# A GRU stack with a feed-forward stage: the feed-forward features by tokens for a whole batch, its weights made in pieces during the stack, the first fusions among the last tails

## What is computed

```python
def _mingru(x, Wz, bz, Wh, bh):
    z = sigmoid(einsum('bsi,hi->bsh', x, Wz) + bz)
    h_tilde = tanh(einsum('bsi,hi->bsh', x, Wh) + bh)
    return _linear_scan(clip(1.0 - z, 1e-8, 1.0 - 1e-8), z * h_tilde)
# 4 layers: h = layernorm(_mingru(h) + (h if i > 0 else 0), gamma, beta); Wz = Wh = ctx[i], bz = bh = cond[i]
x = x + fusion(concat(forward stack, flip(backward stack)))        # 1024 -> 512, of layernorm(x)
gamma = mean(abs(W)) + 1e-6
absmean(W) = sign(W / gamma) * minimum(round(abs(W / gamma)), 1)   # -1, 0 or 1
h = gelu(einsum('btd,hd->bth', layernorm(x), absmean(W_fc)))       # 512 -> 2048
x = x + einsum('bth,dh->btd', layernorm(h, ln_w, ln_b), absmean(W_proj))
```

## Time and profile before

| | |
|---|---|
| median of 3 runs | 1803.64 us (1803.44 to 1804.62) |
| the profiled execution | 1806.48 us |
| its span, first to last instruction | 1804.1 us |
| mean granted TensorE clock | 0.966 |
| TensorE, VectorE, ScalarE, GpSimd busy | 92%, 73%, 53%, 44% of the span |
| the GRU stack's products | 28 to 1009 us |
| first product of `fc` | 1097 us |

### The profile page before, as it was taken

One profiled execution on the slowest core, in us unless ns is written; L12 is line 12 of the kernel. 1 busy time (PEld: TensorE's weight loads), 2 busy tenths in 40 slices (PEclk: granted clock), 3 DMA queues, 4 the chain that ended last, 5 costly groups with the idle time before them and its releaser, 6 DMA issues.

```text
span 1804.1 us, 24288 instructions
## 1 busy us (share of the span) xinstructions
PE 1660.4 (92%) x8448; PEld 1365.1 (76%) x8448; DVE 1324.2 (73%) x2405; ACT 959.5 (53%) x1588; POOL 798.8 (44%) x842
## 2 busy tenths in 40 slices
PE   4779999999799999999999449999999999999999
PEld 3768787877678778777777336888888888888887
DVE  3678889898689989899899468666555555555565
ACT  4367888988578788887977302222222222222222
POOL 2247776767567678675777334111111111111110
PEclk9789999999899999999999768999999999999999
DMA  4000121200010100101001252111111111111100
GB/s 175 1 1 13 36 96 40 100 30 13 21 50 24 48 1 1 71 24 54 1 13 59 85 172 64 47 48 47 47 49 51 49 49 51 50 53 49 48 30 18
DMA packets 62727, 84.67 MB, mean 47 GB/s; under 512 B 3984, under 2 KB 36752, under 8 KB 60432
## 3 DMA queue, kind: packets, MB, share of 16 engines
q1 hardware_dynamic: 58144, 75.01, 12.5%
q10 hardware_dynamic: 4464, 8.13, 1.5%
HBM read 57.95 MB, written 25.17 MB: 46 GB/s over the span
## 4 chain that ended last, share of the span: by engine, by line
PE 56%; DVE 19%; ACT 13%; POOL 6%; issue 5%; DMA 1%; SPq 0%; POOLq 0%; ACTq 0%; DVEq 0%
PE ps L460 13%; PE ps L431 13%; PE ps L333 11%; PE ps L405 10%; DVE bnp L691 4%; ACT ntok L536 4%; PE ps L447 3%; DVE AL L706 3%; ACT H L558 3%; POOL rsp L968 2%; PE ps L367 2%; POOL hb L951 2%; DVE zb L673 2%; ACT AH L563 2%; DVE ps L660 2%
## 5 line engine op out<-in xcount | busy, mean ns | idle before, releaser
L333 PE MATMUL ps<-AH,WH 128*128 128x512 f32 x896 | 373.3, 417 | 29.6 <-DVE AL L706 15.5
L951 POOL TENSOR_TENSOR hb<-zb,hb 128x512 f32<-128x512 f32 x224 | 291.5, 1302 | 145.6 <-ACT hb L525 145.5
L333 PE MATMUL ps<-AL,WH 128*128 128x512 f32 x896 | 354.9, 396 | 0.0
L333 PE MATMUL ps<-AH,WL 128*128 128x512 f32 x896 | 354.4, 396 | 0.0
L673 DVE TENSOR_TENSOR_SCAN zb<-ps,hb 128x512 f32<-128x512 f32 x192 | 234.2, 1220 | 49.0 <-POOL hb L951 43.6
L960 POOL TENSOR_TENSOR H<-H,zb 128x512 f32<-128x512 f32 x192 | 247.9, 1291 | 18.5 <-DVE zb L673 11.7
L629 ACT ACTIVATE uth<-ps 128x512 fp32r<-128x512 f32 x128 | 72.9, 596 | 327.4 <-PE ps L447 327.4
L884 DVE TENSOR_TENSOR utl<-ps,uth 128x512 fp32r<-128x512 f32 x128 | 85.4, 689 | 190.4 <-ACT uth L629 190.3
L333 PEld LDWEIGHTS ps<-AH,WH 128*128 128x128 f32 x896 | 171.6, 192 | 68.4 <-DVE AL L706 17.0
L536 ACT ACTIVATE ntok<-ps,nbp,rsp 128x512 f32<-128x512 f32 x256 | 185.8, 781 | 66.2 <-POOL nbp L971 65.7
L367 PE MATMUL ps<-ident,ntok 128*128 128x128 f32 x1152 | 170.2, 285 | 45.1 <-ACT ntok L536 24.1
(11 more groups left out here) (119 smaller groups left out, 3268.9 us busy)
## 6 DMA issues: line engine op xcount, KB each, us to landing
hs_scratch<-H SPq DMA_DIRECT2D x16, 1024.0 KB, 4.9
hc<-hs_scratch SPq DMA_DIRECT2D x32, 512.0 KB, 4.3
xr<-in_x SPq DMA_DIRECT2D x32, 256.0 KB, 4.3
out<-ob SPq DMA_DIRECT2D x32, 256.0 KB, 2.1
xbuf<-in_x SPq DMA_DIRECT2D x7, 1024.0 KB, 7.1
RAW<-in_wt SPq DMA_DIRECT2D x16, 256.0 KB, 5.7
stg<-in_pjt ACTq DMA_DIRECT2D x16, 256.0 KB, 2.6
stg<-in_fct ACTq DMA_DIRECT2D x15, 256.0 KB, 2.9
```

Of the source, the lines that this page charges most:

```text
L333: r = e.matmul(GATE[i % 3][:], w[:, q, m * 128:(m + 1) * 128], a[:, q, :], start=(n == 0), stop=(n == 11))
L951: e.tensor_tensor(hb[c][:], zb[c][:], hb[c][:], ALU.mult).then_inc(s_p, 1)
```

## The change

The GRU stack keeps its jobs and their order; the order of the other work in a slot is new on every engine. The 40 weight pieces are made one a slot from slot 14 on, into three small buffers `res`, and put to DRAM (`wfu`, `wfc`, `wpj`); whole matrices are loaded back near the end of the stack. The feed-forward stage goes over batches of 512 tokens: `fc(j)` has the weights as stationary operand and gives 128 hidden features by 512 tokens, which is what `proj(j)` needs as stationary operand, so GELU's output isn't transposed. The sums over the 2048 features are kept as running sums of g and of its square over the 16 chunks, and summed over partitions by products with a column of ones (`moments`). The mean is subtracted behind the second layer, with the column sums of the weights (`columns`, `spread`, `shifted`). `hidden` and `evacuate` run on ScalarE, `low_part`, `total` and `ternary` on VectorE, `squares` and `sign` on GpSimd. The fusions of the next batch stand at chunks 2, 5, 8 and 11, the first two (`fuse(0)`, `fuse(1)`) in slots 57 and 58.

```diff
+FUSE_AT = (2, 5, 8, 11)
+NPREP = 40
+PREP0 = 14
+MADE = [2 * n if n < 8 else n + 8 for n in range(NPREP)]
-FEAT_SLOT = [("x", 0, 0), ("f", 3, 1), ("b", 4, 3), ("f", 3, 0), ("b", 4, 2), ("b", 4, 0), ("f", 3, 3), ("f", 3, 2),
...
+FEAT_SLOT = [("b", 4, 1), ("b", 4, 2), ("b", 4, 3), ("f", 3, 2), ("f", 3, 0), ("x", 0, 0), ("x", 0, 3), ("b", 4, 0),
...
+        def fc(j):
+            b, c = j // NC, j % NC
...
+            for q in range(KC):
+                for a in (xh, xl):
+                    r = e.matmul(HIDDEN[j % 2][:], FC[q][:, c * 128:(c + 1) * 128], a[b % 2][:, q, :], start=(n == 0),
+                                 stop=(n == 7))
-        def hid(u, n):
...
-            for m in range(4):
-                c = n * 512 + m * 128
-                r = e.transpose(PS[5 + i % 3][:, m * 128:(m + 1) * 128], g[u % 2][:, c:c + 128], ident[:])
+        def proj(j):
+            b, c = j // NC, j % NC
+            e.wait_ge(f_hi, j + 1)
+            e.wait_ge(f_lo, j + 1)
...
+            for t in range(4):
+                if b > 0 and c == 0:
+                    e.wait_ge(f_ev, 4 * b - 3 + t)
+                for a in (gh, gl):
+                    r = e.matmul(PROJ[t][:], a[j % 3][:, t * 128:(t + 1) * 128], PJ[c], start=(c == 0 and a is gh),
+                                 stop=(c == NC - 1 and a is gl))
+        def moments(b):
...
+            for t in range(4):
+                e.matmul(TURNED[:, t:t + 1], acc[b % 2][:, t * 128:(t + 1) * 128], ones[:], start=True, stop=True)
+            for t in range(4):
+                r = e.matmul(TURNED[:, 4 + t:5 + t], acq[b % 2][:, t * 128:(t + 1) * 128], ones[:], start=True, stop=True)
+        for j in range(NB * NC):
+            b, c = j // NC, j % NC
+            fc(j)
+            if b > 0 and c == 1:
+                moments(b - 1)
+            if b + 1 < NB and c in FUSE_AT:
+                fuse(4 * b + 4 + FUSE_AT.index(c))
+            if j >= 2:
+                proj(j - 2)
+            if j == 3:
+                columns()
+            if j == 9:
+                spread()
+            if b + 1 < NB and c - 2 in FUSE_AT:
+                feat(4 * b + 4 + FUSE_AT.index(c - 2))
+        def hidden(j):
...
+            e.activation(g[j % 2][:], HIDDEN[j % 2][:], ACT.Gelu).then_inc(f_g, 1)
...
+            e.activation(gh[j % 3][:], g[j % 2][:], ACT.Copy, scale=wcol[:, c:c + 1]).then_inc(f_hi, 1)
+            if j >= 1:
+                e.wait_ge(f_s2, j)
+            e.activation(sq[:], g[j % 2][:], ACT.Square).then_inc(f_sq, 1)
+        def evacuate(u):
...
+            e.activation(ob[t][:], PROJ[t][:], ACT.Copy, scale=rg[:, b % 2, t:t + 1]).then_inc(f_ev, 1)
+        def low_part(j):
...
+            e.scalar_tensor_tensor(gl[j % 3][:], g[j % 2][:], wcol[:, c:c + 1], gh[j % 3][:].bitcast(F32), ALU.mult,
+                                   ALU.subtract).then_inc(f_lo, 1)
+        def total(j):
...
+            e.tensor_tensor(acc[b % 2][:], acc[b % 2][:], g[j % 2][:], ALU.add).then_inc(f_s1, 1)
+        def squares(j):
...
+            e.tensor_tensor(acq[b % 2][:], acq[b % 2][:], sq[:], ALU.add).then_inc(f_s2, 1)
+        def ternary(n):
+            r = MADE[n]
+            e.wait_ge(s_pl, n + 1)
+            e.scalar_tensor_tensor(res[r % 3][:], raw[n % 2][:], nth[:, (n - 8) // 16:(n - 8) // 16 + 1],
+                                   res[r % 3][:].bitcast(F32), ALU.is_lt, ALU.subtract, reverse1=True).then_inc(s_pd, 1)
-            if 52 <= s < 56:
-                made(2 * (s - 52))
-                made(2 * (s - 52) + 1)
-            if s == 56:
-                for n in range(8, 13):
-                    made(n)
+        def sign(n):
...
+            e.tensor_scalar(res[r % 3][:], raw[n % 2][:], th[:, w:w + 1], None, ALU.is_gt).then_inc(s_pl, 1)
...
+            value(job(s - 2), 1)
+            add(job(s - 2), 0)
+            aside(s - 1)
+            value(job(s - 2), 2)
...
+            if s == 47:
...
+                e.dma_start(FUH[:].bitcast(F32), wfu[0]).then_inc(d_fu, 16)
...
+                load_unit(2)
+                e.wait_ge(s_mm, 4 * NJ)
+                for i in range(4):
+                    if i == 1:
+                        load_unit(3)
+                    dst = (PJA, PJB)[i // 2][:, 4 * (i % 2):4 * (i % 2) + 4, :]
+                    e.dma_start(dst.bitcast(F32), wpj[:, 4 * i:4 * i + 4, :]).then_inc(d_pj[i], 16)
```

More of the change, by code:

```diff
@@ L195, in pixart_block @@
     hb = [sb(p1, f"hb{i}", [128, S]) for i in range(3)]
+    xbuf1 = sb(p3, "xbuf1", [128, 4, 512])
+    p3.close()
+    raw = [raw0, sb(p1, "raw1", [128, 512])]
+    res = [sb(p1, f"res{i}", [128, 512], F32R) for i in range(3)]
     p1.close()
+    xh = [sb(p2, "xh0", [128, KC, S], F32R)]
+    wcol = sb(p2, "wcol", [128, NC])
+    bcol = sb(p2, "bcol", [128, NC])
+    wb = sb(p2, "wb", [128, NC, 4], F32R)
+    cbc = sb(p2, "cbc", [128, KC, 4])
+    rows = sb(p2, "rows", [128, 2, KC])
+    nmu = sb(p2, "nmu", [128, 2, 4])
@@ new lines, in _ @@
+        e.wait_ge(s_c, 2)
+        for s in SLOTS:
+            if s == 1:
+                shift()
+            tokens(tail_b(s - 3), 1)
+            tokens(tail(s - 2), 1)
+            mm(job(s), 0)
+            back("h", tail_b(s - 3), 2)
+            back("h", tail_b(s - 3), 1)
+            mm(job(s), 1)
+            back("h", tail_b(s - 3), 3)
+            if s == 57:
+                fuse(0)
+            if s == 58:
+                fuse(1)
+                feat(0)
+            back("h", tail(s - 2), 2)
+            back("h", tail_b(s - 3), 0)
+            back("h", tail(s - 2), 0)
+            back("x", batch(s + 1), 0)
+            back("x", batch(s + 1), 3)
+            back("h", tail(s - 2), 1)
+            back("x", batch(s + 1), 1)
+            mm(job(s), 2)
+            back("x", batch(s + 1), 2)
+            back("h", tail(s - 2), 3)
+            tokens(tail(s - 1), 0)
+            mm(job(s), 3)
+            tokens(tail_b(s - 1), 0)
@@ L652, in _ @@
+        for t in range(4):
+            evacuate(NU - 4 + t)
     @block.vector
@@ L943, in _ @@
+        deviation(NB - 1)
+        for t in range(4):
+            shifted(NU - 4 + t)
+        for u in (NU - 2, NU - 1):
+            e.wait_ge(f_ev, u + 1)
+            e.wait_ge(f_xb, u + 1)
+            e.tensor_tensor(ob[u % 4][:], ob[u % 4][:], x1[u % NX1][:], ALU.add).then_inc(f_last, 1)
     @block.gpsimd
@@ L1056, in _ @@
+        inv_2(NB - 1)
+        for t in range(2):
+            final(NU - 4 + t)
     @block.sync
```

1006 lines of the change are left out of this document (526 added, 480 removed).

## The result

The changed kernel takes 1734.62 us (median of 4 runs, 1732.73 to 1734.96) where the kernel before takes 1804.13 (4 runs beside them): a ratio of 0.961, 95% interval 0.9593 to 0.9627. The span of the profiled execution fell from 1804.1 to 1732.8 us, by 71.3. The forecast was 93 less; 1734.6 lies inside its range of 1684 to 1742 and 24 us above its likeliest value.

A forecast was written before the change was run, and what follows sets the result against it. TensorE alone was taken to bound the feed-forward stage, with three engines close to full in the stack. Feed-forward -37, join -48 and stack -8 gave -93, and 2.8 less for the median: 1711 us, range 1684 to 1742.

The forecast's parts named there:

- The join, -48 forecast: Between stack and first layer: ready weights and earlier fusions cut 89.3 us to about 41, -48 us.
- half for three fusions (+5.7): In the join: half clock part of the time makes three fusions 7.4 us instead of 5.5, +5.7 us.
- The stack, -8 forecast: GRU stack: old pieces removed -6, new pieces +5, slot order -7; sum -8 us, from -35 to +45.
- The slot order was entered as -7: GRU stack: new slot order on all engines shortens the way to the next layer, -7 of 67 us TensorE idle.
- The pieces were entered as +5: GRU stack: a tenth of GpSimd's 60 us of piece work, ahead of the scan's gate product, gets through, +5 us.
- the removal of the old pieces: End of the GRU stack: five first-layer weight pieces on VectorE ahead of a gate and its scan go, -6 us.
- The rival with the pieces on the stack's path: GRU stack: GpSimd's comparison delays the gate product the scan waits for, +45 us, 1756 us; chance 0.12.
- The feed-forward stage, -37 forecast: Last stage: earlier fusions -10.9, fewer transposes -57.6, added work +31.5, longer end +2.7, start -2; sum -37 us.
- the check of the other engines: Feed-forward stage: per chunk ScalarE under 2.4 us, VectorE 1.5, GpSimd's addition 1.31, all under TensorE's 3.6 on average.
- the slower case: Feed-forward stage: GELU, copy, low part exceed the 5.4 us that 24 products cover; at 7 us, 1916 us; chance 0.02.
- that sign: GRU stack: the prediction is wrong if VectorE's scan waits much longer for GpSimd's product from slot 14 on.
- That the transposes give back half: Feed-forward stage: removed transposes overlap with products, giving back 29 us and not 58, 1740 us; chance 0.02.

The follow-up runs named there:

- the two later places in the slot: Changed kernel with the weight piece later in the slot on GpSimd and VectorE, 1787.12 us; the same with GpSimd's layer-norm power ahead of the piece, 1781.34 us.
- VectorE's half alone: Changed kernel with the weight piece moved behind the scan and 1 - z on VectorE only, GpSimd's comparison left in place: 1748.10 us, ratio 0.9683.
- the kernel with both moves: Changed kernel with column sums apart, squares summed on VectorE, and the weight piece moved later in the slot on GpSimd and VectorE: 1785.9 us, ratio 0.9885.

## Why the prediction was near, and where it was off

*The join, -48 forecast, -52.4 measured: right, by the steps given.* The weights come ready, two fusions stand among the last tails (one starts at 1009.04), and the first layer begins 37.3 us after the stack. The clock, which I had expected at half for three fusions (+5.7), was 1.00 to 1040, and fell only in the wait for the fourth unit (windows of TensorE: length, busy us and products, clock, DMA share, GB/s):

```profile
1030.00:1040.00 10.00, 9.07 (x44) 1.00 1.02 366
1040.00:1050.00 10.00, 5.85 (x17) 0.66 0.21 68
```

That is the difference of 4.4 us, and a little more.

*The stack, -8 forecast, +0.7 measured: all three of its terms were mis-sized, two of them badly.* The slot order was entered as -7 "without a row for it"; alone it costs 10. The pieces were entered as +5; they cost 7.7. That leaves the removal of the old pieces, for which I had taken only the five in front of the last scan (-6). From the run with the new order alone (1017.7) to the run without computed pieces (1000.3) are 17.4 us: that difference holds the removed pieces and all else in which the two kernels differ ahead of that point, and its parts are not told apart. The sum happened to be only 9 off because errors of opposite sign met: +17.4 for the order, +2.7 for the pieces, -11.4 for what went. That is luck. The prices also don't stand by themselves, since with the pieces in the slots the new order is worth 50 us more than the old one. The rival with the pieces on the stack's path had the right mechanism and the wrong size at the place where the change put them: 45 us were its price, and 7.7 were paid. About its 45 us came where the pieces stood elsewhere: 52 and 51 us at the two later places in the slot, 15 of them with VectorE's half alone, and 50 in the old order. GpSimd is idle for 28% of the stack's time in the changed kernel and for a third of it with the piece moved; its free share said nothing about what one more instruction costs.

*The feed-forward stage, -37 forecast, -19.6 measured: the step that failed is the check of the other engines.* It took VectorE's chunk as 0.77 + 0.77 from rows in which GpSimd was nearly idle (98 of 600 us in the earlier trace rows) and gave GpSimd an addition per chunk in the same sum. Both prices hold only apart. The 17.4 us by places:

- the operations of VectorE are late: 85.03 - 83.77 = 1.26 us a batch, over seven batches 8.8. Without GpSimd's additions the batch takes the time that the prediction's own sum gives (83.6) to 0.2 us;
- column sums 15.5 and not 11.7: +3.8. With the sums apart the clock does not fall behind them, and 6.7 us come back;
- in the last batch, where no fusion covers the copies of the accumulators, 3.5 us were forecast. TensorE stood 3.01 us between two starts, and the next ten steps were slow, at 0.43 us for seven of them: 4.5 us, +1.0;
- the end: from the first product with the column of ones in the last batch to the end it is 13.4 us, where the forecast's terms give 1.9 for the moments, 1.8 for eight products and 5.9: +3.8. Here the eight last products stand 0.43 us apart and the copies wait for them. In the seven runs where those products stand 0.23 apart the stretch still takes 12.4 to 12.8 us. There the way goes from the moments over the deviation, the power on GpSimd (1.03 us) and VectorE's scaling of the column sums (`shifted`, three operations in 2.5 us) to the last additions. The forecast of 5.9 had only copies, an addition and the store, so about 3 of the 3.8 us are this way and under 1 is the clock.

That adds up to 17.4, but to the digit only by chance: smaller terms of both signs are left out. The forecast's own terms add up to -36.3 and not to -37, a batch is 0.2 us longer than its sum even without GpSimd's additions, and of the 3.6 us that it left in for the start of the stage 1.8 came. The removed transposes were priced right (0.11 against 0.104 to 0.11). The wait in the last batch, on the timeline of TensorE:

```profile
1663.45 0.39 PE L459 MATMUL ps<-xl,FCB 128*128 128x512 f32 x1
1666.46 0.47 PE L477 MATMUL ps<-PJA,gh 128*128 128x512 f32 x1 [2.62 <-ACT ob L703]
```

The last products of the changed kernel, on the timeline:

```profile
1720.34 1.03 PE L490 MATMUL ps<-ones,acq 128*128 128x1 f32 x8
1721.23 0.59 PE L477 MATMUL ps<-PJB,gh 128*128 128x512 f32 x1
...
1724.18 0.63 PE L477 MATMUL ps<-PJB,gl 128*128 128x512 f32 x1
```

*The remaining rivals.* TensorE never waited in each chunk for the high or low part, so the slower case did not arise; the cover of 24 products was enough even with VectorE at half its pace. VectorE's scan waited 38.6 us for GpSimd's product of the gates between 200 and 950 us, against 37.3 before, so that sign did not come either. That the transposes give back half falls with the run that put them back.

*What stays open.* Why a piece at the end of a slot costs 38 us more on GpSimd than ahead of the third product: the waits move with every exchange (power, residual, gate product), so no single one is the cause. A place behind the third product or ahead of the second was not tried. Why the clock stayed low for 18 us at the start of the last stage in the kernel with both moves isn't shown either: the portions of column sums in that stretch are the candidate, but the kernel was not run without them. Why the clock fell at the end in some kernels is open too. In nine kernels TensorE waited 0.3 us for `acc` ahead of the last 16 products with the column of ones; the clock fell in or soon behind them in five and in four it didn't. In the three without that wait it didn't fall. So the wait alone does not decide it.

## What to carry to other kernels

A price for an operation of VectorE with its inputs in SBUF holds for the share of time in which GpSimd is idle: before work is split between the two, look at the same operation in a stretch where both run, and consider giving all of it to the faster one. A piece of side work in a stage where three engines take turns is priced by its place and not by the engine's free share; if the place is right it costs a little, a few instructions away it cost about its length in every slot (60 us for 40 pieces of 1.6 us or less), and the move should be measured alone. Bursts of narrow products cost twice, by themselves and in the wide products behind them; in portions of sixteen between wide ones the full clock held where it was up when they began, and in the one profile where it was still at half it stayed there over two portions.

## What the hardware showed that I had not expected

- VectorE's fp32 addition of 512 columns takes 0.68 us alone and 1.77 beside an addition of GpSimd, which itself takes 1.63 to 1.74; the normalisation `n`, with a single large SBUF input, goes from 0.54 to 1.52. Moving GpSimd's addition to VectorE lowered VectorE's busy time in 600 us from 452 to 403.
- TensorE's granted clock fell inside 64 products of four columns, between the 24th and the 32nd, and 12 wide products passed before it was at 2.4 GHz again. In the changed kernel 16 products of one column did not lower it in the seven batches where other work follows; at the end it was at half behind them, and this differs between kernels with the same code there.
- On GpSimd the sum over partitions in slot 22 of the stack takes 13 us out of the engine's work. It takes 0.41, with 5.70 of nothing ahead of it and 6.95 behind it. On the timeline of GpSimd:

```profile
404.29 0.41 POOL L1112 PARTITION_ALL_REDUCE tot<-ssum  x1 [5.70 <-issue]
411.65 1.25 POOL L1106 TENSOR_TENSOR res<-raw,res 128x512 fp32r<-128x512 f32 x1 [6.95 <-issue]
```
